# Opening of a two-layer transformer kernel: weight splits moved to GpSimd, one layer norm moved behind the second layer's units, warm-up products on TensorE

## The reference

```python
# layer 0
scale, shift = split(t_emb @ W_ada.T + b_ada)
h = layernorm(x) * (1 + scale) + shift
q = h @ Wq.T                       # 16 heads of 32
c_kv = h @ Wkd.T                   # latent of 128
k, v = c_kv @ Wku.T, c_kv @ Wvu.T  # 4 heads of 32
x = x + softmax(mask(rope(q) @ rope(k).T / sqrt(32))) @ v @ Wo.T
# layer 1
h = rmsnorm(x) * (w1 * (1 + t_emb @ tw1.T))
x = x + softmax(rope(h @ Wq.T) @ rope(h @ Wk.T).T / 8) @ (h @ Wv.T) @ Wo.T
h = rmsnorm(x) * (w2 * (1 + t_emb @ tw2.T))
x = x + (silu(h @ Wg.T) * (h @ Wu.T)) @ Wd.T   # inner width 2048
```

## Time and profile before

| | |
|---|---|
| median of 3 runs | 1804.07 us (1800.82 to 1804.49) |
| profiled execution, span from first to last instruction | 1804.9 us |
| PE busy | 1717.2 us (95%), 12440 matmuls |
| DVE busy | 1152.3 us (64%) |
| ACT busy | 945.9 us (52%) |
| POOL busy | 398.8 us (22%) |
| mean DMA traffic | 130 GB/s |

### The profile page before, as it was taken

The page is one execution under the profiler, slowest core; times in us unless marked ns, Lnnn a source line. Parts: engine busy times, 40 slices in busy tenths (PEclk is TensorE's granted clock), DMA queues, the critical chain, the costliest instruction groups (busy, mean ns, idle before and its releaser), DMA issues.

```text
span 1804.9 us, 37773 instructions
## 1 busy us (share of the span) xinstructions
PE 1717.2 (95%) x12440; PEld 931.9 (52%) x12440; DVE 1152.3 (64%) x2858; ACT 945.9 (52%) x2769; POOL 398.8 (22%) x556
## 2 busy tenths in 40 slices
PE   6686899999999999999999999999999999999999
PEld 2344445555455545555455554555455554555444
DVE  6759566675667657685576756676576855767320
ACT  3836456364664538564483646645385644835320
POOL 3438587011111112111110111111121111101120
PEclk9676999999999999999999999999999999999999
DMA  7866489462784449662593637944485725936220
GB/s 245 152 181 115 126 197 253 98 117 82 163 175 94 80 119 184 133 118 78 127 194 91 119 88 161 171 95 82 115 192 125 123 73 138 196 85 112 100 70 24
DMA packets 527231, 234.30 MB, mean 130 GB/s; under 512 B 476336, under 2 KB 493744, under 8 KB 527024
## 3 DMA queue, kind: packets, MB, share of 16 engines
q1 hardware_dynamic: 511472, 175.09, 48.9%
q10 hardware_dynamic: 15552, 56.63, 10.1%
HBM read 90.09 MB, written 16.78 MB: 59 GB/s over the span
## 4 chain that ended last, share of the span: by engine, by line
PE 77%; DVE 10%; DMA 6%; issue 4%; ACT 2%; SPq 1%; DVEq 0%; POOL 0%; ACTq 0%
PE up L1427 8%; PE up L1429 8%; PE up L1428 8%; PE gate L1427 7%; PE gate L1429 7%; PE gate L1428 7%; PE y L1427 4%; PE y L1428 4%; PE y L1429 4%; PE bank L1427 4%; PE bank L1429 4%; PE bank L1428 4%; DMA prob_t<-prob 3%; PE bank L1454 2%; DVE prob L1113 2%
## 5 line engine op out<-in xcount | busy, mean ns | idle before, releaser
L864 ACT ACTIVATE bank<-bank,low 128x128 f32<-128x128 f32 (+2 forms) x768 | 302.7, 395 | 68.2 <-DVE low L1106 35.0
L702 POOL TENSOR_TENSOR inner_t<-inner,inner_t 128x512 f16<-128x512 f32 x128 | 149.0, 1164 | 662.7 <-ACT inner_t L1045 662.6
L1113 DVE TENSOR_TENSOR prob<-bank,prob 128x512 f16<-128x512 f32 (+1 forms) x320 | 202.8, 634 | 54.3 <-ACT prob L873 53.4
L873 ACT ACTIVATE prob<-bank 128x512 f16<-128x512 f32 (+1 forms) x320 | 178.7, 558 | 73.3 <-DMA prob_t<-prob 44.5
L1427 PE MATMUL up<-mlp,ring 128*128 128x512 f16 x512 | 194.9, 381 | 12.8 <-DVE inner L1392 12.8
L1382 DVE SCALAR_TENSOR_TENSOR silu<-silu,gate 128x512 f32<-128x512 f32 x128 | 87.9, 687 | 183.8 <-ACT silu L1039 183.0
L1427 PE MATMUL gate<-mlp,ring 128*128 128x512 f16 x512 | 194.0, 379 | 1.4 <-DVE mlp L1078 0.9
L1429 PE MATMUL up<-mlp,ring 128*128 128x512 f16 x512 | 194.9, 381 | 0.0
L1428 PE MATMUL up<-mlp,ring 128*128 128x512 f16 x512 | 194.9, 381 | 0.0
L1429 PE MATMUL gate<-mlp,ring 128*128 128x512 f16 x512 | 194.0, 379 | 0.0
L1428 PE MATMUL gate<-mlp,ring 128*128 128x512 f16 x512 | 193.9, 379 | 0.0
(11 more groups left out here) (182 smaller groups left out, 4041.8 us busy)
## 6 DMA issues: line engine op xcount, KB each, us to landing
ring<-wgu_dram ACTq DMA_DIRECT2D x108, 512.0 KB, 3.8
x_in<-x_dram SPq DMA_DIRECT2D x18, 512.0 KB, 3.8
x_res<-x_mid SPq DMA_DIRECT2D x16, 512.0 KB, 3.0
wgu_dram<-ring SPq DMA_DIRECT2D x16, 512.0 KB, 3.6
out_dram<-x_res SPq DMA_DIRECT2D x32, 256.0 KB, 2.3
prob_t<-prob SPq DMA_TRANSPOSE x256, 3.5
inner_t<-wd_t_dram SPq DMA_DIRECT2D x4, 1024.0 KB, 8.7
ring<-wg_t_dram SPq DMA_DIRECT2D x16, 256.0 KB, 4.1
```

The costliest lines, as they stand in the source:

```text
L702: pool.tensor_tensor(inner_t[:, 1, f, :], inner[:], inner_t[:, 0, f, :], ALU.subtract).then_inc(inner_low, 1)
L864: ins = act.activation(bank_[:, at:at + wid], bank_[:, at:at + wid], ACT.Exp, bias=low[:, j % BANKS, k:k + 1], scale=-1.0, accum_out=total)
L873: act.activation(terms(prob[:, g % SLOTS, 0, :], layer, j), terms(work_bank[USE[f"unit{layer}", j] % BANKS][:], layer, j), ACT.Copy).then_ ...
L1113: dve.tensor_tensor(terms(prob[:, slot, 1, :], layer, j), terms(work_bank[USE[name] % BANKS][:], layer, j), terms(prob[:, slot, 0, :], lay ...
```

## The change: what it does

Three parts, nearly all in the first round.

1. *Who splits.* Wq0 and Wo0 join the matrices that GpSimd splits whole. GpSimd's opening list is now: roots of the layer norm, low parts of "kv" (scaling, then subtraction), Wq0, the angles, the halved identity and mask; at `fill0.0`, after the tables of the angles, Wq1, Wo1, Wo0 and wkv1. The wait of Wq1 for `stack_low` is gone. ScalarE keeps the high parts of "kv" alone; VectorE splits no weight. ScalarE's sine of the first angles moves from the start to the step `keys.0`, behind the keys' high parts.
2. *Layer norm.* In the opening, the first sequence is normalised right after its statistics, the second between the two row copies. In the first round, the statistics for the next pair move from units 3 and 5 of layer 1 to `out1a`, ahead of the first residual add, and the normalisation from units 7 and 9 to `heads1`, ahead of the last heads' low parts; GpSimd's roots move to `out1a.0` and `out1a.1`. The later rounds keep the old places.
3. *Warm-up.* TensorE waits for the identity and runs 36 products of 128x256 in float16 on it, into a bank that nothing reads, before it waits for the condition vector.

```diff
+START_STATS = {"out1a.0": 0, "out1a.1": 1}
-PIECE, DVE_PIECES = 512, 6
-PIECES_AT = {"first": range(0, 2), "lat.0": range(2, 6), "unit0_9": range(6, 7), "unit0_11": range(7, 8),
-             "unit0_14": range(8, 9), "unit0_16": range(9, 10), "unit0_18": range(10, 11)}
-BIG = ["wq1", "wo1"] + [f"wd{c}" for c in range(CH)]
-SPLIT_AT = {"fill0.0": BIG[:2], "kv1.0": BIG[2:5], "unit1_6": BIG[5:]}
+PIECE = 512
+BIG = ["wq0", "wq1", "wo1", "wo0"] + [f"wd{c}" for c in range(CH)]
+SPLIT_AT = {"fill0.0": BIG[1:4], "kv1.0": BIG[4:7], "unit1_6": BIG[7:]}
+WARM = 36
-ANGLES_AT, SINES_AT = "unit1_6", "end"
+ANGLES_AT, SINES_AT, START_SINES_AT = "unit1_6", "end", "keys.0"
...
 # gpsimd
+            def piece_low(piece):
+                pool.wait_ge(raw_high, piece + 1)
+                parts = list(zip(piece_views(piece, 0), piece_views(piece, 1)))
+                for (src, _), _ in parts:
+                    ins = pool.tensor_scalar(src, src, WS, 1.0, ALU.mult, ALU.mult)
+                ins.then_inc(raw_scaled, 1)
+                pool.wait_ge(raw_scaled, piece + 1)
+                for (src, hi), (_, lo) in parts:
+                    ins = pool.tensor_tensor(lo, src, hi, ALU.subtract)
+                ins.then_inc(raw_split, 1)
...
+                        if step == "fill0.0":
+                            piece_split(KV1_PIECE)
...
-                    if step in LN_STATS:
-                        ln_root((n[0], n[1] + 1), LN_STATS[step])
+                    stats = LN_STATS if m is not None else START_STATS
+                    if step in stats:
+                        ln_root((n[0], n[1] + 1), stats[step])
...
-                if key == "wq1":
-                    pool.wait_ge(stack_low, 3 * PAIR)
...
             pool.memset(prob[:], 0.0).then_inc(prob_clear, 1)
+            for s in BOTH:
+                ln_root((None, 0), s)
+            for piece in KV_PIECES:
+                piece_low(piece)
+            big_split_("wq0")
             pool.wait_ge(freq_in, 16)
             angles((None, 0))
-            for s in BOTH:
-                ln_root((None, 0), s)
...
 # scalar
-                        weight_highs(step)
+                        if step == START_SINES_AT:
+                            sines_(n)
...
-            sines_((None, 0))
-            weight_highs("first")
+            kv_highs()
...
 # vector
             def finish(n, m, layer):
                 between(m, f"out{layer}a.0", f"out{layer}a.1")
+                ahead = m is None and layer == 1
+                if ahead:
+                    for s in BOTH:
+                        ln_stats((n[0], n[1] + 1), s)
                 for s in BOTH:
                     add(n, layer, s, 0)
                 for s in BOTH:
                     normalise(n, layer, s, 1)
                 between(m, f"heads{layer}.0", f"heads{layer}.1")
+                if ahead:
+                    for s in BOTH:
+                        ln_apply((n[0], n[1] + 1), s)
                 for s in BOTH:
                     heads_low(n, layer, s, 1)
...
             ln_stats((None, 0), 0)
+            ln_apply((None, 0), 0)
+            ln_stats((None, 0), 1)
             mod_copies(0)
-            ln_stats((None, 0), 1)
+            ln_apply((None, 0), 1)
             mod_copies(1)
-            for s in BOTH:
-                ln_apply((None, 0), s)
             gains(0)
-            weight_lows("first")
...
 # tensor
+            pe.wait_ge(ident_made, 1)
+            warm = ident[:].bitcast(F16)
+            for _ in range(WARM):
+                pe.matmul(gbank[:, 0:2 * P], warm[:, 0:P], warm, start=True, stop=True)
             pe.wait_ge(cond_in, 32)
```

More of the change, by code:

```diff
@@ L363, in build @@
             sem("cond_in"), sem("ln_w_in"), sem("const_in"), sem("pos_in"), sem("freq_in"))
[L364 removed]
+        raw_high, raw_scaled, raw_split = sem("raw_high"), sem("raw_scaled"), sem("raw_split")
         cond_used, cond_copied, cond_turned = (
@@ L422, in build @@
         CONDITIONS = ["ada0", "ada1", "tw1", "tw2"]
-        PIECE_OF = [("kv", wkd, 0, 0, 512), ("kv", wkv0, 0, 512, 256)] + [
-            (key, w, p * PIECE, p * PIECE, PIECE) for key, w, pieces in (
-                ("wq0", wq0, 4), ("wo0", wo0, 4), ("wkv1", None, 1)) for p in range(pieces)]
+        PIECE_OF = [("kv", wkd, 0, 0, PIECE), ("kv", wkv0, 0, PIECE, 256), ("wkv1", None, 0, 0, PIECE)]
+        KV_PIECES, KV1_PIECE = range(2), 2
         def staged(key):
@@ L452, in big_views @@
             slot = staged(key)
-            w, at = ((wq1, 0) if key == "wq1" else (wo1, 0) if key == "wo1" else
-                     (wd, int(key[-1]) * CH))
+            w, at = {"wq0": (wq0, 0), "wo0": (wo0, 0), "wq1": (wq1, 0), "wo1": (wo1, 0)}.get(
+                key, (wd, int(key[-1]) * CH))
             return [(slot[:, c * D:(c + 1) * D], flat(w[half])[:, (at + c) * D:(at + c + 1) * D])
@@ L681, in _, with piece_split @@
             pool.wait_ge(half_made, 1)
+            def piece_low(piece):
[8 more added lines that the diff above has]
+                ins.then_inc(raw_split, 1)
+            def piece_split(piece):
+                pool.wait_ge(*landed[PIECE_OF[piece][0]])
+                for src, hi in piece_views(piece, 0):
+                    ins = pool.tensor_scalar(hi, src, WS, 1.0, ALU.mult, ALU.mult)
+                ins.then_inc(raw_high, 1)
+                piece_low(piece)
             def ln_root(n, s):
@@ L1010, in square, with kv_highs @@
                                accum_out=squares[:, s, t:t + 1]).then_inc(square_sum, 1)
[L1012 to L1015, removed]
-                    act.wait_ge(*landed[PIECE_OF[piece][0]])
+            def kv_highs():
+                act.wait_ge(*landed["kv"])
+                for piece in KV_PIECES:
                     for src, dst in piece_views(piece, 0):
-                        ins = act.activation(dst, src, ACT.Copy, scale=WS)
-                    ins.then_inc(raw_high, 1)
+                        act.activation(dst, src, ACT.Copy, scale=WS).then_inc(raw_high, 1)
             def ring_loads(n, chunks, last=False):
@@ L1132, in between @@
                             gains(1)
-                        weight_lows(step)
             def units(n, m, layer):
@@ L1142, in units @@
                     between(m, step)
-                    if step in LN_STATS:
+                    if m is not None and step in LN_STATS:
                         ln_stats((n[0], n[1] + 1), LN_STATS[step])
-                    elif step in LN_APPLY:
+                    elif m is not None and step in LN_APPLY:
                         ln_apply((n[0], n[1] + 1), LN_APPLY[step])
@@ L1365, in gains @@
                     dve.wait_ge(gains_made, 4 * CH)
-            def weight_lows(step):
-                for piece in PIECES_AT.get(step, ()):
-                    if piece >= DVE_PIECES:
-                        dve.wait_ge(*landed[PIECE_OF[piece][0]])
-                        for src, dst in piece_views(piece, 0):
-                            ins = dve.tensor_scalar(dst, src, WS, None, ALU.mult)
-                        ins.then_inc(raw_high, 1)
-                    dve.wait_ge(raw_high, piece + 1)
-                    for (src, hi), (_, lo) in zip(piece_views(piece, 0), piece_views(piece, 1)):
-                        ins = dve.scalar_tensor_tensor(lo, src, WS, hi, ALU.mult, ALU.subtract)
-                    ins.then_inc(raw_split, 1)
             def gates(n, chunks):
```

1 line of the change is left out of this document (added).

## The result

The kernel after takes **1811.92 us** (median of 9 runs, 1807.99 to 1814.19) against 1804.49 us (1800.82 to 1806.77) for the kernel before: a ratio of 1.0040, 95% interval 1.0031 to 1.0048. The change costs 7.4 us. 1799.5 was forecast, in a range that ended at 1806.5: wrong, and on the other side.

A forecast was written before the change was run, and what follows sets the result against it. TensorE bounds everything after 200 us; before that a single string, then ScalarE's waits, then VectorE set the pace. Terms +0.5 - 2.9 - 3.7 + 1.5 = -4.6 took 1804.1 to 1799.5 us, range 1791.5 to 1806.5.

The forecast's parts named there:

- The step that failed: Rounds after the first 200 us: no instruction altered, so they are only shifted by what the first round gains or loses.
- Warm-up: First half of the conditioning: runs at the second half's pace, 3.60 us instead of 6.38, a gain of 2.8 us.
- Order of layer norm and gains: Opening: second normalisation starts near 15.3 us, VectorE's first cast comes at 21.1 us instead of 23.3.
- toll: Opening: VectorE's casts and subtractions each cost 0.39 us more while GpSimd scales, 0.93 while it subtracts; fill ends at 30.3.
- The first rival, no toll: Opening: overlap with GpSimd costs VectorE's casts and subtractions nothing, -5.7 instead of +0.5 us, total 1793.3; chance 0.22.
- Opening: First round up to the first scores and prob transposes: +0.5 us in sum, slower.
- Units of layer 0: First round, layer 0: VectorE loses weight halves, so ScalarE's 2.9 us wait for minima goes, -2.9 us.
- the second rival's slots: Units of layer 0: places for prob set the pace, not VectorE; gain there only 0.5 us, total 1802.8; chance 0.18.
- Units of layer 1: First round, layer 1: without the next pair's layer norm, ScalarE's waits for minima and slots shrink, -3.7 us.
- Finish: End of layer 1: normalisation ahead of the last head's low part delays it and the projection, +1.5 us; statistics cost nothing.
- GpSimd's roots: End of layer 1: they stand behind GpSimd's other work but are done 1.7 us before VectorE arrives, so hidden.
- The third rival: End of layer 1: GpSimd late with the roots, 10 us late giving +3.7 us, total 1807.8, slower; chance 0.10.

The follow-up runs named there:

- b_pe: The kernel before with 72 instructions of already met waits on TensorE ahead of the conditioning, nothing else: 1814.47 us, ratio 1.0046 to before.
- a_back: The kernel after with met waits that bring the later rounds' code of all four engines back to before's place: 1804.95 us, 0.9997 to before.
- b_ln: The kernel before with only the next pair's statistics and normalisation moved from layer 1's units to the finish: 1806.14 us, 1.0013 to before.
- b_lnlate: As b_ln, but the normalisation stands behind the last heads' low parts instead of ahead of them: 1805.24 us, 1.0004 to before.
- a_noln0: As a_back, with the next pair's statistics and normalisation in the first round's units of layer 1 again: 1801.38 us, 0.9980 to before.
- a_s164: As a_back, with TensorE's code 164 instructions beyond before's place; total time not in the text, layer 1's last probability to next MLP 23.0 us.

## Why the prediction was wrong

- **The step that failed**: "the change alters no instruction of those rounds … The later rounds are shifted by that amount and no more." The first half is true, the second isn't. 36 products ahead of the loop move TensorE's code by 72 instructions, and its blocks are then fetched into other transposes in every round. b_pe (+0.46%) and a_back (from +0.40% back to -0.03%) show it. The sum had no term for it, and no rival had it either.
- **Warm-up**: right, 6.38 to 3.59 us.
- **Order of layer norm and gains, toll**: right. The second normalisation starts at 15.4 (15.3 forecast), the first cast at 21.06 (21.1), the fill ends at 30.3 (30.3). The first rival, no toll, falls.
- **Opening**: +1.9 instead of +0.5, in one profile. TensorE's clock, at the lower level for the latent and key products, is by estimate 1.1 of the difference; the sum had no term for it. Among executions of before's opening (before, b_ln, b_lnlate) the first scores already move by 1.2 us, 47.7 to 49.0.
- **Units of layer 0**: -3.1 for -2.9. ScalarE's wait for the minima fell from 2.9 to 0.6 us, the second rival's slots did not hold it. Opening and these units together were worth 2.4 by the forecast and 1.2 in after's profile; the 3.6 (2.0 to 5.2) of a_noln0 include the opening that its pads made faster.
- **Units of layer 1**: -2.4 for -3.7. The minima's wait fell by 2.5, from 4.8, but the slots' stayed, at 1.9 after 1.7:

```profile
ACT bank L883 <- DVE low L1122: 2.3, 2, 2.0
ACT prob L892 <- DMA prob_t<-prob: 1.9, 1, 1.9
```

- **Finish**: mis-sized, +4.9 up to the next round's first MLP product for a forecast of +1.5. The delay of the low parts was nearly right, 1.1 us for 1.5. The projection at half pace behind it was not seen, 2.5 us, and the statistics weren't free: the second residual add comes 0.8 us later against the last probability than in before. With the clock up the whole was +1.8 (a_s164). So this part of the change, forecast at -2.2, is about +2 (b_ln).
- **GpSimd's roots**: hidden, as forecast. The last ends at 175.8, VectorE comes at 178.9. The third rival falls, though it named the slower side.

## What to carry to other kernels

A change ahead of a loop also moves the loop's code. Where a loop's bound hangs on DMAs with little room, price this at what a pad of the same length costs the unchanged kernel, here up to 0.5%, and try a few places of the code before a change of that size is judged: here the place alone lay between a loss of 0.4% and none. Check in the trace that a pad moves nothing but code: ahead of an engine's first instruction it can, as with ScalarE's table load. And where a step adds to a wait of TensorE in a stretch in which it is not kept busy, give the product behind that wait a price at the lower clock too, as a second case: here 5 us instead of 1.8.

## What was not expected of the hardware

- A transpose of the probabilities takes 3.1 us alone and 4.4 to 4.7 when a 16384 B code packet of about 1.0 us falls into it; its first partial landing shifts with its last. That the packet itself causes it is read from their coincidence, unit by unit, in before, b_pe and a_back; how a packet holds up a transpose was not looked into, and a load of the same kind by itself was not tried.
- The granted clock in the first round differs between kernels that do the same work there: at 28 to 30 us it is 0.50 in after and 1.00 in a_noln0, and at the end of layer 1 0.50 in after and 1.00 in a_s164. In the first round's balance, -1.6 us, single terms of -2.9 and +2.5 go with it.
- Three instructions of met waits ahead of ScalarE's opening move its table load from 0.74 to 14.49 us, and the first scores with it, from 50.8 to 48.0 (after, a_back). That the earlier scores come from this is read from the chain in the two traces; no run has that pad alone.
